# A post-norm decoder layer on one core: the quantised feed-forward unrolled into one block, on 16-bit integers and split products

## The chip, the cores and the metric

One core of one Trainium2 chip. The metric is the device time of the whole program, in microseconds (us). Engines go by the names of the profile: PE is TensorE, PEld its weight loads, DVE VectorE, ACT ScalarE, POOL GpSimd, SP SyncE (it issues the transfers here).

## The reference

`x` is 4 x 1024 rows of 256 values. The first two lines below are attention; the change is in the second and third.

```python
x = _layernorm(x + attn(x))              # 16 heads, relative positions
x = _layernorm(x + xattn(x, ctx_1024))   # one head, 154 context rows
x = _layernorm(x + ffn(x))
def act_qdq(x):                          # one scale for the whole tensor
    scale = jnp.maximum(jnp.max(jnp.abs(x)) / 32767, 1e-12)
    return jnp.clip(jnp.round(x / scale), -32768, 32767) * scale
# ffn: 256 -> 768 -> 256, weights of 4 bits with a scale for each 32
x = act_qdq(x)
up = act_qdq(x @ lpbq_dequant(w_up).T)
gate = act_qdq(x @ lpbq_dequant(w_gate).T)
sig = fixed_qdq_u16(jax.nn.sigmoid(gate))    # round to 1/65536, at most 65535/65536
gate = act_qdq(gate * sig)
o = act_qdq(gate * up)
return o @ lpbq_dequant(w_down).T
```

Each of the five `act_qdq` needs the largest absolute value of its whole tensor before the first value can be rounded. So the feed-forward falls into stages with one scale between each and the next.

## The kernel before

Line numbers are those of the profile. The self-attention fills the first 1018 us, and the diff leaves it alone. `decoder_rest` (L842) does what follows, for 8 blocks (`NBLK`) of 512 rows (`HALF`), in four `nc.Block`s, at the end of each of which all engines meet: `cross_attention` (L967), `project_gate` (L1469), `project_up` (L1592) and `down` (L1712). Within a block every engine runs its own list of instructions in order, and semaphores tie the lists. In the last three the lists are hardware loops (`Fori`), so each wait is written with `hold`: a separate wait instruction and a count on `s_held`, ahead of the instruction that it protects. In `cross_attention` the loops are unrolled in Python and a single wait is part of the instruction behind it.

**cross_attention.** Step s works on three blocks of rows at once. PE's list is: project the attention's output (`project_out`, L1336 to L1346), turn the normed rows (`turn_h`, L1355), turn the exponentials (`turn_e`, L1362 and L1365), turn the attention rows of two steps ahead (`turn_at`, L1313 to L1318), turn 512 columns of feed-forward weights (`turn_weights`, L1394), weigh the values (`weigh`, L1378 to L1381), scores (L1384 to L1390). Turns are transposes against an identity, eight of 128 x 128 for a block of rows. All turns share two pairs of PSUM banks in the order of the list `turns`: a turn begins when the copy of the last but one is done (`begin`, L1306). ACT copies each turned tile to SBUF (L1169 to L1171, `copy_e`, `copy_weights`) and does the exponentials (L1198) and the two norms' scaling. DVE adds (L1244, L1247), reduces the scores (L1257), scales and adds (L1268), and takes the largest of the finished rows (L1281). POOL adds the bias (`add_bias`, L1137), gathers tails of the exponentials (L1143), and does the small steps of the norms (`norm_rstd`, L903 to L910, behind DVE's L892 to L900). SP stores the finished rows to DRAM (L1093).

**A scale.** DVE reduces eight maxima to `top` (`largest_of`, L929), POOL reduces over the partitions (`scale_pool`, L950), DVE makes step and inverse (`scale_of`, L931 to L946). `scale_of` of the first scale stands in `project_gate`, so behind the end of the cross-attention's block.

**project_gate.** SP loads the rows again (L1488). A rounding is two steps: ACT scales and adds a magic number (L1504), DVE takes it off and scales back to values (L1536). PE turns the block (`turn`, L1565), ACT copies it (L1508), PE makes 12 fp32 products with 512 columns each for 6 banks (L1574), ACT empties the banks (L1514), DVE takes the maximum (L1540). `raw` holds the gate of all 8 blocks in fp32, `xqT` the turned rows.

**project_up.** PE makes the up products of the same `xqT` (L1708), ACT empties them to `ub` (L1649) and SP stores six of eight blocks to DRAM (L1613). Beside that the gate is rounded (ACT L1630, DVE L1664), ACT takes the sigmoid to `sg` (L1643) and rounds it (L1647), DVE clips it (L1674), multiplies (L1681) and takes the maxima of both (L1683, L1668).

**down.** For each block, the two kept in `ub` first, ACT rounds gate (L1771) and up (L1774, L1777), DVE takes the magic number off (L1794, in every second block), multiplies (L1797) and takes the maximum (L1799), while SP loads the next `ub` (L1742): the multiply stage. Behind the fifth scale ACT rounds (L1782), DVE makes values (`down_in`, L1811), PE makes 24 products of 256 columns (L1840), DVE adds the residual (`finish`, L1817) and norms, and SP writes the result (L1751, L1753): the down stage.

## Time and profile before

| | |
|---|---|
| runs of the kernel | 1586.56 us median of 3 (1586.03 to 1588.25) |
| the profiled execution, its own time | 1586.74 us |
| its span | 1585.0 us, 25411 instructions |
| mean granted clock of TensorE | 0.928 |
| PE busy | 1329.9 us (84%) |
| DVE busy | 1073.5 us (68%) |
| ACT busy | 967.9 us (61%) |
| POOL busy | 277.3 us (17%) |

The profile is of one execution. A line of a timeline is: start in us from the beginning of the span, duration in us, engine, line of the kernel, operation, output<-input with shapes, x how many such in a row were put together; in brackets how long the engine had idled before it, and what ended that. The shares are means over stages with different limits, the self-attention above all, so they say little of the last 570 us; those are read by stretches.

### The profile page before, as it was taken

Reading aid. Unit: us, or ns where it says so; the run is one execution under the profiler, and the core shown is the slowest. Engines: PE = TensorE matmul, PEld = TensorE weight load, DVE = VectorE, ACT = ScalarE, POOL = GpSimd, SP = SyncE. Lnnn points to the kernel's source line nnn. Section 1 sums busy time; section 2 is a strip of 40 time slices with the busy share of each in tenths; the row PEclk is TensorE's granted clock in tenths of the full one; section 3 lists DMA queues with packets and bytes.
Section 4 is the critical chain, followed back from the end, with each engine's and each line's share of the span. In section 5 each row is a group of like instructions: output and inputs, shape, how many; then the busy total and the mean of one; then the engine's idle time right before and its main releaser. Section 6 shows DMA issues by size and latency. Waiting matters only on the chain. (4 is left out here: it accounts for less than half of the span.)

```text
span 1585.0 us, 25411 instructions
## 1 busy us (share of the span) xinstructions
PE 1329.9 (84%) x8028; PEld 652.3 (41%) x8028; DVE 1073.5 (68%) x2571; ACT 967.9 (61%) x1652; POOL 277.3 (17%) x524
## 2 busy tenths in 40 slices
PE   5867799999999999999999999699739988600587
PEld 2433243344334433443344333278624433200576
DVE  4246678877887788778877888237623359979354
ACT  2332477777777777777777777447624478768500
POOL 2332112121212121212121211044300000000011
PEclk8989899999999999999999999899959999955799
DMA  4999786978697879787977770463121002125022
GB/s 107 258 301 303 190 235 196 253 200 235 197 251 202 234 198 251 201 230 202 248 204 225 207 243 17 139 181 111 40 80 40 13 40 119 79 80 185 0 95 90
DMA packets 264618, 264.73 MB, mean 167 GB/s; under 512 B 65934, under 2 KB 250926, under 8 KB 260398
## 3 DMA queue, kind: packets, MB, share of 16 engines
q1 hardware_dynamic: 264494, 263.21, 57.6%
q8 instruction: 61, 1.00, 0.3%
q14 instruction: 63, 0.52, 0.1%
HBM read 151.66 MB, written 110.71 MB: 166 GB/s over the span
## 5 line engine op out<-in xcount | busy, mean ns | idle before, releaser
L537 ACT ACTIVATE pr<-scoresT 128x512 f32<-128x512 f32 x1024 | 551.4, 602 | 217.0 <-PE scoresT L788 158.7
L784 PE MATMUL scoresT<-qT,kT 99*128 99x512 bf16 (+7 forms) x1408 | 358.7, 326 | 7.1 <-DMA qT<-sh 5.3
L639 DVE TENSOR_REDUCE mx<-scores_for_max 128x1 f32<-128x888 f32 (+6 forms) x448 | 301.9, 674 | 0.0
L634 DVE CUSTOM_DVE_ANT_0 junk<-scores_for_max,win 128x200 f32<-128x200 f32 (+2 forms) x512 | 180.2, 352 | 163.4 <-PE scores_for_max L759 156.0
L637 DVE TENSOR_REDUCE mx<-scores_for_max 128x1 f32<-128x64 f32 (+6 forms) x448 | 277.8, 620 | 0.0
L801 PE MATMUL attn_out<-pr,vS 128*17 128x512 f32 x2048 | 269.5, 598 | 0.1
L784 PEld LDWEIGHTS scoresT<-qT,kT 99*128 99x128 bf16 (+1 forms) x1408 | 113.7, 97 | 335.7 <-ACT rows L517 97.8
L788 PE MATMUL scoresT<-idf,win 128*128 128x128 f32 x1024 | 218.2, 274 | 0.0
L1840 PE MATMUL banks<-w_downT,work 128*128 128x256 f32 x384 | 87.5, 392 | 106.2 <-DVE work L1811 106.2
L758 PE MATMUL scores_for_max<-kX,qT 64*128 64x512 bf16 x512 | 165.4, 385 | 11.0 <-DVE mx L639 9.2
L434 POOL COPY rows<-rows 128x736 f32<-128x736 f32 x128 | 102.2, 799 | 398.6 <-ACT rows L517 398.6
L759 PE MATMUL scores_for_max<-kX,qX 64*128 64x512 bf16 x512 | 165.4, 385 | 0.0
L788 PEld LDWEIGHTS scoresT<-idf,win 128*128 128x128 f32 x1024 | 131.9, 143 | 21.8
L1840 PEld LDWEIGHTS banks<-w_downT,work 128*128 128x128 f32 x384 | 75.8, 198 | 118.3 <-issue 107.3
L1708 PE MATMUL banks<-xqT,w_upT 128*128 (+1 forms) x192 | 87.2, 609 | 18.5 <-ACT ub L1649 12.9
L1574 PE MATMUL banks<-xqT,w_gateT 128*128 128x512 f32 (+1 forms) x192 | 85.5, 603 | 0.0
L758 PEld LDWEIGHTS scores_for_max<-kX,qT 64*128 64x128 bf16 x512 | 35.8, 93 | 108.7 <-issue 61.9
L463 POOL TENSOR_TENSOR an<-ov,orec 128x256 f32<-128x256 f32 x32 | 19.9, 622 | 294.6 <-DVE orec L654 189.4
L517 ACT ACTIVATE rows<-scoresT 128x288 f32<-128x288 f32 x128 | 53.5, 418 | 24.5 <-DMA rel_table<-rows 19.3
L1540 DVE TENSOR_REDUCE amax<-raw (+1 forms) x8 | 26.8, 3353 | 60.5 <-ACT raw L1514 60.5
L1708 PEld LDWEIGHTS banks<-xqT,w_upT 128*128 128x128 f32 x192 | 36.4, 194 | 69.3 <-issue 69.2
L1514 ACT ACTIVATE raw<-banks 128x512 f32 (+1 forms) x48 | 28.7, 597 | 46.4 <-PE banks L1574 46.4
(172 smaller groups left out, 1612.7 us busy)
## 6 DMA issues: line engine op xcount, KB each, us to landing
rel_table<-rows SPq DMA_DIRECT2D x128, 512.0 KB, 4.2
win<-rel_table SPq DMA_DIRECT2D x128, 512.0 KB, 5.4
up_raw<-ub SPq DMA_DIRECT2D x6, 1536.0 KB, 5.1
ub<-up_raw SPq DMA_DIRECT2D x6, 1536.0 KB, 6.6
qT<-q_parts SPq DMA_DIRECT2D x32, 256.0 KB, 7.3
kX<-k_parts SPq DMA_DIRECT2D x64, 128.0 KB, 4.8
kT<-k_parts SPq DMA_DIRECT2D x32, 256.0 KB, 5.5
q_parts<-part SPq DMA_DIRECT2D x32, 192.0 KB, 5.5
```

Of the source, the lines that this page charges most:

```text
L434: nc.gpsimd.tensor_copy(rows[:, j, :, 0:LP], rows[:, j, :, LP:LP + 1].to_broadcast([P, G, LP])).then_inc(r_padded, 1)
L537: nc.scalar.activation(pr[:, n % NPR, h, :], bank, ACT.Exp).then_inc(t_read, 1)
L634: last = nc.vector.tensor_tensor_reduce(junk[:, n % 2, 0:z - a], bank[:, a:z], win[:, T % NW, q4, h, u:u + z - a], 1.0, NEG, ALU.add, ALU. ...
L637: last = nc.vector.tensor_reduce(mx[:, T % 2, q4, h, 0:1], bank[:, 0:a], AX.X, ALU.max)
L639: last = nc.vector.tensor_reduce(mx[:, T % 2, q4, h, 2:3], bank[:, z:L], AX.X, ALU.max)
L758: mm(psX[:, n % 2, 0:HALF], qT[0:64, q_slot(i), h, lo:lo + P], kX[0:64, i % 2, h, :], start=True, stop=True)
L759: mm(psX[:, n % 2, HALF:L], qX[64:128, i % 2, h, lo:lo + P], kX[64:128, i % 2, h, :], start=True, stop=True).then_inc(x_full, 1)
L784: last = mm(bank[:, a:e], k[0:r], q[0:r, a:e], start=(n == 0), stop=not near and n == len(pieces) - 1, skip_group_check=True)
L788: last = mm(bank[:, q4 * P:(q4 + 1) * P], side, idf[:], is_transpose=True, start=False, stop=n == len(near) - 1, skip_group_check=True)
L801: last = mm(psO[32 * h:32 * h + VW, :], vS[:, i % 2, kt, VW * h:VW * (h + 1)], pr[:, n % NPR, h, :], start=(kt == 0), stop=(kt == TL - 1))
L1708: last = nc.tensor.matmul(ps[:, m, :], wuT[:, c, m * P:(m + 1) * P], xqT[:, c, bass.ds(n, 1), :].rearrange("p a n -> p (a n)"), start=(c = ...
L1840: last = nc.tensor.matmul(ps[:, 2 * par + q // 2, (q % 2) * D:(q % 2 + 1) * D], work[:, par, m * HALF + q * P:m * HALF + (q + 1) * P], wdT ...
```

## The change

The three blocks of the feed-forward become one, `feed_forward`, unrolled in Python, with plain waits in place of `hold`. In it:

- The turn of the rows moves into the cross-attention, `turn_x(n)` behind `turn_at` of step n + 3, the last three behind the main loop; it turns the rows before they are rounded, to `xr`, [128, 2, 8, 512] in fp32. SP's store of the rows stays (the residual of the last norm needs it); the load for the gate goes. The first scale is made in the cross-attention's block.
- A rounding is one step: ACT scales and writes a 16-bit integer (`xi`, `gi`, `si`, `ui`). Steps and inverses are multiplied in where a later instruction scales anyway.
- Gate and up products are three products of type float32r on halves of the operands: rows and weights are each split into a high part (a copy of type float32r) and the rest, and low x high, high x high and high x low go to the same bank. The weights are split by POOL in the cross-attention (`split_weights`), the rows by DVE ahead of the gate (`split_rows`) and again by POOL for the up products (`split_again`), since only two blocks of halves are kept.
- All eight banks take products in turn, in place of six.
- The sigmoid is scaled by DVE into an unsigned 16-bit integer, which replaces the clip, the rounding on ACT and the taking-off.
- In the down stage the products stay fp32; the block is unrolled and double-buffered as before.
- POOL gets a spare all-reduce at the start of the cross-attention.

```diff
-        wuT = sb("w_upT", [P, 2, FI])
-        wgT = sb("w_gateT", [P, 2, FI])
+        wuh = sb("w_up_high", [P, 2, FI], F32R)
+        wul = sb("w_up_low", [P, 2, FI], F32R)
+        wgh = sb("w_gate_high", [P, 2, FI], F32R)
+        wgl = sb("w_gate_low", [P, 2, FI], F32R)
...
+            nc.gpsimd.partition_all_reduce(spare[:], neg_half[:], P, RMAX)
...
+            def split_weights(j):
+                pool.wait_ge(w_whole, j + 1)
+                nc.gpsimd.tensor_copy(high, wt[:, j % 2]).then_inc(w_high, 1)
+                pool.wait_ge(w_high, j + 1)
+                nc.gpsimd.tensor_tensor(low, wt[:, j % 2], high.bitcast(F32), ALU.subtract).then_inc(w_low, 1)
...
+                    split_weights(s - 2)
                 if s + 2 < NBLK:
...
+                if j < 6:
+                    if j >= 2:
+                        act.wait_ge(w_low, j - 1)
...
-                    copy(f"at{s + 2}", pair(atT[:]))
+                    copy(f"at{s + 2}", atT[:])
+                if 3 <= s <= NBLK:
+                    copy(f"x{s - 3}", xr[:, :, s - 3, :])
...
+            dve.wait_ge(d_am, NBLK)
+            largest_of(dve, 0)
+            scale_of(dve, 0, d_link, 0)
...
+            def turn_x(n):
+                pe.wait_ge(d_h2, n + 1)
+                to = begin(f"x{n}")
+                for c in range(2):
+                    for q in range(4):
+                        last = tr(to[:, c, q * P:(q + 1) * P], h2[:, n % 2, q, c * P:(c + 1) * P], idf[:])
+                last.then_inc(t_turned, 1)
...
+                if s >= 3:
+                    turn_x(s - 3)
...
+        xi = sb("x_int", [P, 2, NBLK, HALF], I16)
+        xh = sb("x_high", [P, 2, 2, HALF], F32R)
+        xl = sb("x_low", [P, 2, 2, HALF], F32R)
+        gi0 = sb("g_int", [P, FT * HALF], I16)
+        si = sb("s_int", [P, FT * HALF], U16T)
...
+            for n in range(NBLK - 2):
+                sp.wait_ge(f_out, M_ALL + FT * (n + 1))
+                sp.dma_start(ud[n], ub[n % 2]).then_inc(u_st[n % 2], 16)
...
+            def split_again(n):
+                pool.wait_ge(f_full, M_ALL + FT * (n - 1))
+                for c in range(2):
+                    k = 2 * n + c
+                    if k:
+                        pool.wait_ge(f_xu, k)
+                    nc.gpsimd.tensor_copy(x_one, xi[:, c, n, :]).then_inc(f_x1, 1)
+                    pool.wait_ge(f_x1, k + 1)
+                    nc.gpsimd.tensor_copy(xh[:, n % 2, c], x_one).then_inc(f_x2, 1)
+                    pool.wait_ge(f_x2, k + 1)
+                    nc.gpsimd.tensor_tensor(xl[:, n % 2, c], x_one, xh[:, n % 2, c].bitcast(F32), ALU.subtract).then_inc(f_xu, 1)
+            pool.wait_ge(f_xg, NBLK)
+            split_again(0)
+            scale_pool(pool, 1)
+            split_again(1)
+            for n in range(2, NBLK):
+                split_again(n)
+            scale_pool(pool, 2)
+            scale_pool(pool, 3)
...
+            def round_rows(n):
+                nc.scalar.activation(xi[:, :, n, :], xr[:, :, n, :], ACT.Identity, scale=inv[:, 0:1]).then_inc(f_xi, 1)
+            def empty(k, to):
+                act.wait_ge(f_full, k + 1)
+                nc.scalar.activation(to, ps[:, k % BANKS, :], ACT.Identity, scale=step[:, 0:1]).then_inc(f_out, 1)
...
+            def round_gate(n):
+                if n >= 2:
+                    act.wait_ge(f_g2, n - 1)
+                nc.scalar.activation(gi[n % 2], raw[:, n, :], ACT.Identity, scale=inv[:, 1:2]).then_inc(f_gi, 1)
...
+            def sigmoid(n):
+                act.wait_ge(f_gi, n + 1)
+                nc.scalar.activation(raw[:, n, :], gi[n % 2], ACT.Sigmoid, scale=step[:, 1:2]).then_inc(f_sig, 1)
+            def empty_up(n, first, last):
+                if first == 0 and n >= 2:
+                    act.wait_ge(u_st[n % 2], 16 * (n // 2))
+                    act.wait_ge(f_umax, n - 1)
+                for m in range(first, last):
+                    empty(M_ALL + FT * n + m, ub[n % 2][:, cols(m)])
...
+            round_rows(0)
+            round_rows(1)
+            for n in range(NBLK):
+                if n + 2 < NBLK:
+                    round_rows(n + 2)
+                for m in range(FT):
+                    empty(FT * n + m, raw[:, n, cols(m)])
+            act.wait_ge(t_inv, 2)
+            round_gate(0)
+            for n in range(NBLK):
+                sigmoid(n)
+                empty_up(n, 0, FT // 2)
+                if n + 1 < NBLK:
+                    round_gate(n + 1)
+                empty_up(n, FT // 2, FT)
+            for k, n in enumerate(ORDER):
+                if k == 0:
+                    act.wait_ge(t_inv, 3)
+                if k >= 2:
+                    act.wait_ge(f_o, k - 1)
+                nc.scalar.activation(gi[k % 2], raw[:, n, :], ACT.Identity, scale=inv[:, 2:3]).then_inc(f_g2i, 1)
+                if k == 0:
+                    act.wait_ge(t_inv, 4)
+                if n not in KEPT:
+                    act.wait_ge(u_ld[n % 2], 16 * (n // 2 + 1))
+                nc.scalar.activation(ui[k % 2], ub[n % 2], ACT.Identity, scale=inv[:, 3:4]).then_inc(f_ui, 1)
+            act.wait_ge(t_inv, 5)
+            for n in range(NBLK):
+                nc.scalar.activation(raw[:, n, :], raw[:, n, :], ACT.Identity, bias=magic[:, 0:1], scale=inv[:, 4:5]).then_inc(o_r, 1)
...
+            def split_rows(n):
+                dve.wait_ge(f_xi, n + 1)
+                if n >= 2:
+                    dve.wait_ge(f_full, FT * (n - 1))
+                nc.vector.tensor_copy(xh[:, n % 2], xi[:, :, n, :]).then_inc(f_xh, 1)
+                dve.wait_ge(f_xh, n + 1)
+                nc.vector.tensor_tensor(xl[:, n % 2], xi[:, :, n, :], xh[:, n % 2].bitcast(F32), ALU.subtract).then_inc(f_xg, 1)
...
+            def largest_up(n):
+                dve.wait_ge(f_out, M_ALL + FT * (n + 1))
+                largest(3, n, ub[n % 2], f_umax)
+            split_rows(0)
+            split_rows(1)
+            for n in range(NBLK):
+                dve.wait_ge(f_out, FT * (n + 1))
+                if n + 2 < NBLK:
+                    split_rows(n + 2)
+                largest(1, n, raw[:, n, :], f_gmax)
+            dve.wait_ge(f_gmax, NBLK)
+            largest_of(dve, 1)
+            scale_of(dve, 1, f_link, 0)
+            dve.wait_ge(t_inv, 2)
+            nc.vector.tensor_scalar(coarse[:, 0:1], step[:, 1:2], 1.0 / U16, None, ALU.mult).then_inc(f_link, 1)
+            for n in range(NBLK):
+                dve.wait_ge(f_sig, n + 1)
+                nc.vector.tensor_scalar(si[:], raw[:, n, :], U16, None, ALU.mult).then_inc(f_si, 1)
+                dve.wait_ge(f_si, n + 1)
+                nc.vector.tensor_tensor(raw[:, n, :], gi[n % 2], si[:], ALU.mult).then_inc(f_g2, 1)
+                if n:
+                    largest_up(n - 1)
+                dve.wait_ge(f_g2, n + 1)
+                largest(2, n, raw[:, n, :], f_g2max)
+            dve.wait_ge(f_g2max, NBLK)
+            largest_of(dve, 2)
+            largest_up(NBLK - 1)
+            scale_of(dve, 2, f_link, 2, coarse[:, 0:1])
+            dve.wait_ge(f_umax, NBLK)
+            largest_of(dve, 3)
+            scale_of(dve, 3, f_link, 5)
+            dve.wait_ge(t_inv, 4)
+            nc.vector.tensor_tensor(coarse[:, 1:2], step[:, 2:3], step[:, 3:4], ALU.mult).then_inc(f_link, 1)
+            for k, n in enumerate(ORDER):
+                dve.wait_ge(f_ui, k + 1)
+                nc.vector.tensor_tensor(raw[:, n, :], gi[k % 2], ui[k % 2], ALU.mult).then_inc(f_o, 1)
+                dve.wait_ge(f_o, k + 1)
+                largest(4, n, raw[:, n, :], f_omax)
...
+            down_in(0)
+            down_in(1)
+            for n in range(NBLK):
+                finish(n)
+                if n + 2 < NBLK:
+                    down_in(n + 2)
...
+                for m in range(FT):
+                    k = first + FT * n + m
+                    if k >= BANKS:
+                        pe.wait_ge(f_out, k - BANKS + 1)
+                    cols = slice(m * P, (m + 1) * P)
+                    terms = [(w[:, c, cols], v[:, n % 2, c]) for w, v in ((low, xh), (high, xh), (high, xl)) for c in range(2)]
+                    for t, (w, v) in enumerate(terms):
+                        last = mm(ps[:, k % BANKS, :], w, v, start=(t == 0), stop=(t == len(terms) - 1))
+                    last.then_inc(f_full, 1)
+            for n in range(NBLK):
+                pe.wait_ge(f_xg, n + 1)
+                project(0, n, wgh, wgl)
+            for n in range(NBLK):
+                pe.wait_ge(f_xu, 2 * n + 2)
+                project(M_ALL, n, wuh, wul)
+            pe.wait_ge(f_out, 2 * M_ALL)
+            for n in range(NBLK):
+                pe.wait_ge(o_q, n + 1)
+                if n >= 4:
+                    pe.wait_ge(l_sum, 2 * NBLK + n - 3)
```

## Rows read from the trace of the kernel before

**Rows 1.** Stretches: busy us and operations of PE, PEld, DVE, ACT, POOL; PEclk, DMA, GB/s.

```profile
1184.65:1274.30 89.65, 89.65 (x241) 41.99 (x240) 27.53 (x13) 41.52 (x60) 0.00 (x0) 0.98 0.10 30
1290.01:1394.60 104.59, 77.20 (x175) 31.90 (x173) 101.53 (x39) 81.79 (x69) 0.00 (x0) 0.95 0.22 91
1408.16:1473.40 65.24, 0.00 (x0) 0.00 (x0) 60.36 (x20) 48.42 (x17) 0.00 (x0) 0.50 0.45 161
1480.08:1573.80 93.72, 87.50 (x384) 75.76 (x384) 42.85 (x98) 17.77 (x7) 11.94 (x28) 0.93 0.23 73
1066.00:1165.00 99.00, 80.44 (x484) 66.60 (x481) 59.08 (x218) 61.20 (x147) 38.66 (x68) 0.91 0.25 75
```

**Rows 2.** The timeline of one step of the cross-attention, PE and ACT.

```profile
1081.83 2.36 PE L1390 MATMUL banks<-kq,h1T 128*128 128x154 f32 x16
...
1090.82 1.02 ACT L1171 ACTIVATE atT<-banks 128x1024 f32<-128x1024 f32 x1 [0.50 <-PE banks L1318]
...
1093.94 2.13 PEld L1390 LDWEIGHTS banks<-kq,h1T 128*128 128x128 f32 x16 [0.33 <-issue]
```

**Rows 3.** The timeline of PE: two bf16 passes, gate products, a turn.

```profile
600.10 0.39 PE L758 MATMUL scores_for_max<-kX,qT 64*128 64x512 bf16 x1
...
600.32 0.38 PE L758 MATMUL scores_for_max<-kX,qT 64*128 64x512 bf16 x1
...
1184.65 12.43 PE L1574 MATMUL banks<-xqT,w_gateT 128*128 128x512 f32 x24
...
1197.78 10.46 PE L1574 MATMUL banks<-xqT,w_gateT 128*128 128x512 f32 x24
...
1208.09 1.04 PE L1565 MATMUL banks<-ident_f,hb 128*128 128x128 f32 x8
```

**Rows 4.** The timeline of POOL in the self-attention: a subtraction and a copy.

```profile
23.13 1.15 POOL L430 TENSOR_TENSOR part<-rem,part 128x512 bf16<-128x512 f32 x1 [20.75 <-ACT part L505]
...
69.23 0.80 POOL L434 COPY rows<-rows 128x736 f32<-128x736 f32 x1
```

**Rows 5.** The timeline where POOL changes between its own operations and the all-reduce.

```profile
1030.07 2.35 POOL L1137 TENSOR_TENSOR xt<-xt,bot 128x1024 f32<-128x1024 f32 x1 [11.08 <-DMA xt<-x]
...
1035.84 1.22 DVE L1247 TENSOR_TENSOR h<-banks,xt 128x1024 f32<-128x1024 f32 x1 [21.19 <-PE banks L1346]
...
1167.62 0.16 DVE L929 TENSOR_REDUCE top<-amax 128x1 f32<-128x8 f32 x1 [2.22 <-PEq L976]
...
1174.31 0.38 POOL L950 PARTITION_ALL_REDUCE top_all<-top  x1 [12.36 <-issue]
...
1278.95 0.35 POOL L950 PARTITION_ALL_REDUCE top_all<-top  x1 [104.27 <-DVE top L929]
...
1496.56 0.38 DVE L900 BATCH_NORM_AGGREGATE mean_var<-stats 128x2 f32<-128x6 f32 x4
...
1504.06 0.25 POOL L905 TENSOR_SCALAR rstd<-mean_var 128x4 f32<-128x4 f32 x1 [30.02 <-issue]
```

**Rows 6.** The timeline of ACT at the start and the end of the up stage.

```profile
1285.80 1.28 ACT L1643 ACT_TABLE_LOAD   x1
...
1384.63 2.86 ACT L1647 ACTIVATE sg<-sg,magic 128x3072 f32<-128x3072 f32 x1 [4.03 <-DVE sg L1674]
...
1387.39 1.55 ACT L1649 ACTIVATE ub<-banks 128x512 f32<-128x512 f32 x3
```

**Rows 7.** The timeline of DVE in a block of the up stage.

```profile
1355.82 1.75 DVE L1674 TENSOR_SCALAR sg<-sg 128x3072 f32<-128x3072 f32 x1
...
1362.47 3.35 DVE L1681 SCALAR_TENSOR_TENSOR raw<-sg,raw 128x3072 f32 x1
...
1366.06 3.35 DVE L1683 TENSOR_REDUCE amax<-raw  x1 [0.24 <-DVE raw L1681]
```

**Rows 8.** The down stage: PE in the timeline, then the last link of the chain.

```profile
1509.91 10.32 PE L1840 MATMUL banks<-w_downT,work 128*128 128x256 f32 x40 [6.18 <-DVE work L1811]
...
1509.91 63.86 PE banks L1840 x288
```

More of the change, by code:

```diff
@@ L1055, in cross_attention @@
         turns += [f"w{j}" for j in range(NBLK - 1, W_GROUPS)]
+        turns += [f"x{n}" for n in range(NBLK - 2, NBLK)]
         turn_of = {name: n for n, name in enumerate(turns)}
@@ L1240, in _ @@
                         copy_weights(j)
+            for n in range(NBLK - 2, NBLK):
+                copy(f"x{n}", xr[:, :, n, :])
         @block.vector
@@ L1717, in down @@
-def down(nc, sem, hold, tokens, h2d, ud, wdT, magic, coarse, t_coarse, step, inv, t_inv, ps, raw, ub, amax,
-         largest_of, scale_of, scale_pool, l_sum, norm_stats, norm_rstd, norm_apply, out):
-    with ExitStack() as ctx:
-        work = ctx.enter_context(nc.sbuf_tensor("work", [P, 2, FT * HALF], F32))
-        res = ctx.enter_context(nc.sbuf_tensor("res", [P, 2, 4, D], F32))
-        p_ld = [sem(f"p_ld{j}") for j in range(2)]
-        p_g = sem("p_g")
-        p_gi = sem("p_gi")
-        p_odd = sem("p_odd")
-        p_u = sem("p_u")
-        p_o = sem("p_o")
-        p_a = sem("p_a")
+            for n in range(NBLK - 2, NBLK):
+                turn_x(n)
@@ L1736, in down, with wait, rows_of @@
         block = ctx.enter_context(nc.Block())
+        def wait(eng, s, value):
+            eng.wait_ge(s, value)
+        def rows_of(t, n):
+            return t[n].rearrange("(q p) d -> p q d", p=P)
         @block.sync
         def _(sp):
[L1740 to L1746 removed]
@@ L1779, in _ @@
-            run_kept_first(act, multiply)
-            act.wait_ge(t_inv, NSC + 1)
-            with act.Fori(0, NBLK) as n:
-                nc.scalar.activation(flat(raw, n), flat(raw, n), ACT.Identity, bias=magic[:, 0:1], scale=inv[:, 4:5]).then_inc(o_r, 1)
+            def round_rows(n):
[3 more added lines that the diff above has]
+                nc.scalar.activation(to, ps[:, k % BANKS, :], ACT.Identity, scale=step[:, 0:1]).then_inc(f_out, 1)
@@ L1832, in _, with project @@
+            down_in(0)
[4 more added lines that the diff above has]
+                    down_in(n + 2)
         @block.tensor
         def _(pe):
-            def products(n, par, before):
-                hold(pe, o_q, n + 1)
-                if before:
-                    hold(pe, l_sum, 2 * NBLK + n - 1)
+            mm = nc.tensor.matmul
+            def project(first, n, high, low):
+                for m in range(FT):
[7 more added lines that the diff above has]
+                    last.then_inc(f_full, 1)
```

483 lines of the change are left out of this document (142 added, 341 removed).

## The prediction

> **What bounds the kernel now.** I read the share of each stage first, then the order of time inside each, then what ended the waits. The change leaves the first 1018 us (the self-attention) as they are, so the question is the rest. The table of stretches [rows 1] shows five kinds of work there. In the cross-attention PE is busy 80 of 99 us, more than any other engine. In the gate products it is busy all 89.65 us. In the up products DVE is busy 101.5 of 104.6 us and PE only 77. In the multiply stage PE has nothing and DVE 60 of 65 us. In the down products PE is busy 87.5 of 93.7 us. Between them lie hand-offs, in which nearly all engines wait for one scale. So three stages end with PE and two with DVE, and what each edit is worth is read in its own stage.
>
> **Cross-attention, with the rows turned there.** A step lasts 12.1 us, from scores to scores [rows 2]. Eight transposes end to end take 1.04 us, so eight more cost 8 x 0.11 = 0.9 us of PE per step [rows 3]. The turn of the weights now also waits for the copy of `at` (1.02 us), beside which the new turn runs: 0.4 more. Steps 3 to 7 give 5 x 1.3, step 8 about 1.0: **+7.5**. Ends: 5.3 (transposes alone) and 11 (each copy shows as well). ACT's extra copy lies beside PE's work, and so do POOL's weight splits, 0.6 + 1.15 each [rows 4]; without that cover each would cost its own length, up to 1.8 a step. The two last turns and the store of the rows run beside the scale below.
>
> **POOL's turn between its own operations and the all-reduce.** The scale of the rows shows a price with no engine behind it [rows 5]: `top` starts at 1167.62, the all-reduce only at 1174.31. The first small operation after the all-reduces starts at 1504.06, though its input was there at 1497. Between all-reduces there is none: that at 1278.95 starts as its `top` ends. I read this as 6.6 to 6.8 us for each turn of POOL from the one kind to the other, paid when POOL comes to it; an instruction's own single wait lies behind it, so it can pass beside a wait, which a separate held wait forbids. The Trainium skill, GPSIMD Engine Reference, Instruction dispatch, says that the first call to a freshly loaded kernel costs about 6 us that no instruction shows; by its figure each turn is 0.7 us cheaper than I take. The new spare all-reduce at 1019 then brings two turns, to 1033, and the first bias ends at 1035.4 in place of 1032.4. DVE's first sum starts at 1035.84 and waits for PE: cost 0, or a few us if the turns are longer.
>
> **Hand-off to the gate.** Before: POOL's last small operation ends at 1161.95 (1174.31 - 12.36), the first product starts at 1184.65 [rows 3]: 22.7. After: POOL turns at once, beside the second norm (6.6), all-reduce 0.4, step and inverse 0.5, end of the block 0.5, rounding of 1024 columns 1.1 (from 2.86 for 3072 [rows 6]), copy 0.7 and subtraction 1.2 on DVE (from 1.75 and 3.35 for 3072 [rows 7]), semaphores 0.5: 11.5. The load, the second rounding step and the turn have gone. **-11.2**.
>
> **Gate.** Now a product is two instructions of 0.43 us for 512 columns (24 in 10.46 [rows 3]); with eight transposes a block takes 11.2. After: 36 products a block of the new type. The trace doesn't show it; the nearest rows are bf16 at 0.22 us (600.10 to 600.32) and the 4-byte instruction at 0.43. I take 0.22: a full product takes two instructions of twice 0.22, which is four combinations of halves, and the change writes out three of these four itself, on values cut to one half. Against it speaks that a 4-byte transpose takes 0.11 for 128 columns, the rate of 0.43. The Trainium skill, FP8 and Floating Point Precision, TensorE Precision Notes, counts true fp32 as four passes, high and low of both operands, and the trace's 4 x 0.215 agrees; by it a product is 0.215 and the gate 1.4 us shorter than I take. The weights' loads hide, since transposes with a load each follow at 0.11. 288 x 0.22 = 63.4, and 2.0 for the start at the lower clock, as the first block pays today (12.43 against 10.46): 65.4 against 89.65, **-24.3**. DVE (0.7 + 1.2 + 3.35) and ACT (1.1 + 6 x 0.6) stay under the 7.9 of PE. If the loads show, 0.25 to 0.27 a product, +9 to +14.
>
> **Hand-off to the up stage.** POOL starts its first split one block before the gate's end G, at G - 7.9: two copies 1.2, a turn 6.8, subtraction 1.2, the other half 2.6; done at G + 4. Then the turn back 6.6 and the all-reduce, G + 11.0, though `top` is there at G + 4.2. Inverse G + 11.5, rounding 2.9, table 1.3, sigmoid 2.9 [rows 6]: DVE starts at G + 18.8. Today it is 1290.01 - 1274.30 = 15.7: **+3.1**.
>
> **Up stage.** DVE per block after: scaling 1.75, a product of 3.35 behind a gap of 0.15 to 0.24, two maxima of 3.3 [rows 7]: 11.7. One scaling (1.8) has gone; the product keeps its length, as its output stays 4 bytes wide. First block 9.1, then 7 x 11.7: 91.0 against 104.6, **-13.6**. ACT (2.8 + 2.9 + 6 x 0.6) and PE (7.9) stay under it. New is POOL beside DVE, splitting again: 2 x (0.6 + 0.6 + 1.15) and waits, 5.2 us a block [rows 4]. No row shows the two side by side on such work. Ends: 0, and all 5.2. I take 0.5, as DVE's maxima (6.6 of 11.7) leave POOL room: **+3.5**.
>
> **To the multiply stage.** DVE's first product waits for two passes of ACT, not three, and no block ends: 13.6 becomes 10.1, **-3.5**. **Multiply stage.** DVE 3.5 + 3.4 a block; ACT's 2 x 2.8 is under it and the loads of `ub` have two blocks to land. 55.3 against 65.2, **-9.9**. The hand-off to the down stage stays.
>
> **Down stage.** POOL now meets its turn ahead of the wait for the statistics, so the 6.18 us in which PE stands at 1509.91 go. The unrolled code may shorten the block (63.86 / 6 = 10.64 [rows 8]); for that I take 1.0: **-7.2**. Next late is DVE, 9.1 of 10.6 a block, no bound yet.
>
> **Sum.** 7.5 - 11.2 - 24.3 + 3.1 - 13.6 + 3.5 - 3.5 - 9.9 - 7.2 = -55.6. The profiled execution took 1586.74 (span 1585.0), 0.2 over the median of the runs, too little to matter: 1586.7 - 55.6 = 1531.
>
> **Rivals.** *A: a product of the new type streams like any 4-byte operand, 0.43 us.* For it: every 4-byte row does. Against: the count of halves. Gate 288 x 0.21 = +60.4. Up: a block is 15.5 us of PE, over DVE's 11.7; from G + 18.8, with eight banks ahead, 40 groups of 2.58 end at G + 122 and the last maximum at G + 126, where it was G + 117: +9.5. Total 1601, slower. With the up stage the point from which it decides is 0.40 us a product.
> *B: DVE and POOL shut each other out, so that all 5.2 us of POOL's block stand in DVE's way.* Against: POOL needs under half of the block. 7 x 4.7 = +33: 1564. The Trainium skill, SBUF — State Buffer, SBUF: two separate sides, speaks for it: VectorE with two SBUF inputs or in a two-port mode and GpSimd exclude each other for a whole instruction. No row here shows that.
> *C: the 6.7 us are paid once per kind, not at each turn.* Then the spare call has paid: the rows' scale comes 3 us earlier, the gate's 6.3: 1522. Against: 1504.06 is an operation that POOL had done all through the cross-attention.
> *D: it doesn't do what it says*: the splits wait for buffers and the stages keep their length, 1587.
>
> **How the numbers follow.** Forecast case 0.66, A 0.18, B 0.08, C 0.06, D 0.02. The time is that of the first. Its own range is 1518 to 1550: cross-attention -2 to +3.5, product 0.215 to 0.27, POOL 0 to 1 us a block, hand-offs 3 either way. The range for all, 1516 to 1566, takes in B and C and leaves out A and D, 0.20. A measurement of this kernel can tell about 0.2% (3 us) from no change. Faster by more: 0.66 + 0.08 + 0.06 = 0.80; the same 0.02; slower 0.18.
>
> **What would show it.** 36 single products of a block in 7.9 us and a gate stage of 64 to 67; the all-reduce of the gate's scale 6 us behind its `top`; DVE 11.7 us a block in the up stage, 6.9 in the multiply stage, with no waits for ACT or PE; no hole of PE in the down stage; a cross-attention step of 13.4. Products 0.43 us apart would make it wrong outright; DVE operations that start late or last longer than 3.35 us while POOL splits would be B.

## The result, and the profile after

Median of 4 runs 1525.44 us (1523.96 to 1526.34) against 1587.4 us of the kernel before, measured beside it; ratio 0.9608, 95% interval 0.9591 to 0.9625: faster by 3.9%. The profiled execution took 1525.12 us, its span 1523.2. Forecast were 1531 and a range of 1516 to 1566.

The span falls apart into stages by the same marks in both traces: POOL's first memset, the end of its last small operation in the cross-attention, PE's first and last gate product, DVE's first scaling, the reduction to `top` behind the up stage, the first product of the multiply stage, the next reduction to `top`, PE's first and last product of the down stage, the end.

| stage | before, us | after, us | difference | forecast |
|---|---|---|---|---|
| self-attention, up to the memset | 1018.08 | 1016.72 | -1.4 | 0 |
| cross-attention | 143.87 | 148.97 | +5.1 | +7.5 |
| hand-off to the gate | 22.70 | 10.07 | -12.6 | -11.2 |
| gate | 89.65 | 67.87 | -21.8 | -24.3 |
| hand-off to the up stage | 15.71 | 17.87 | +2.2 | +3.1 |
| up stage | 104.55 | 96.24 | -8.3 | -13.6 + 3.5 |
| hand-off to the multiply stage | 13.60 | 9.73 | -3.9 | -3.5 |
| multiply stage | 65.27 | 53.35 | -11.9 | -9.9 |
| hand-off to the down stage | 6.65 | 6.43 | -0.2 | 0 |
| down stage | 93.68 | 86.03 | -7.7 | -7.2 |
| tail | 11.24 | 9.92 | -1.3 | 0 |
| span | 1585.0 | 1523.2 | -61.8 | -55.6 |

The stretches of the changed kernel that answer to [rows 1], the cross-attention last again (columns as there):

```profile
1175.76:1243.63 67.87, 67.83 (x288) 55.61 (x288) 36.22 (x21) 37.09 (x54) 1.22 (x2) 0.96 0.00 0
1261.50:1357.70 96.20, 63.66 (x252) 50.92 (x252) 93.44 (x31) 67.05 (x62) 54.66 (x40) 0.82 0.28 109
1367.47:1420.78 53.31, 0.00 (x0) 0.00 (x0) 53.04 (x16) 38.84 (x14) 0.00 (x0) 0.50 0.49 177
1427.25:1513.28 86.03, 86.03 (x384) 74.95 (x384) 42.93 (x98) 17.80 (x7) 11.94 (x28) 0.97 0.25 80
1064.70:1165.70 101.00, 85.42 (x539) 72.44 (x537) 58.20 (x217) 64.54 (x149) 49.64 (x80) 0.96 0.25 74
```

The bounds are where they were: PE in the gate (67.83 of 67.87 us) and in the down stage (no hole any more), DVE in the up stage (93.44 of 96.20) and in the multiply stage, where it now has next to no gap. New is POOL in the up stage, 54.66 us busy beside DVE.

PE in a step of the cross-attention, to be read against [rows 2], and the first products of the gate stage beside some at full clock, against [rows 3]; the timeline:

```profile
1080.50 2.36 PE L1414 MATMUL banks<-kq,h1T 128*128 128x154 f32 x16
1089.29 1.04 PE L1423 MATMUL banks<-ident_f,h 128*128 128x128 f32 x8
1090.66 0.63 PE L1437 MATMUL banks<-ident_f,wn 128*128 128x128 f32 x4 [0.33 <-ACT atT L1180]
1094.01 2.36 PE L1414 MATMUL banks<-kq,h1T 128*128 128x154 f32 x16
...
1175.76 1.22 PE L1748 MATMUL banks<-x_high,w_gate_low 128*128 128x512 f32 x2 [5.86 <-DVE x_low L1663]
1176.78 1.05 PE L1748 MATMUL banks<-x_high,w_gate_high 128*128 128x512 f32 x2
...
1185.40 0.62 PE L1748 MATMUL banks<-x_high,w_gate_high 128*128 128x512 f32 x2
1185.86 0.62 PE L1748 MATMUL banks<-x_low,w_gate_high 128*128 128x512 f32 x2
```

A step is 13.51 us (1080.50 to 1094.01) where it was 12.11: the turn at L1423 and 0.33 us of wait for the copy of `at` ahead of the next one. A pair of split products starts every 0.455 us: 0.227 a product, no longer 0.436 for each half of an fp32 one. The first five pairs run at the lower of the clock's two levels, 0.85 a pair; PE had stood still for 5.86 us before them. The granted clock was 0.50 in 1176 to 1180 and 1.00 from 1181 on.

POOL's timeline around the two hand-offs, against [rows 5]:

```profile
1165.49 0.20 POOL L904 TENSOR_TENSOR shift<-shift,rstd 128x4 f32<-128x4 f32 x1
1171.51 0.38 POOL L946 PARTITION_ALL_REDUCE top_all<-top  x1 [5.82 <-issue]
1235.58 0.61 POOL L1579 CAST xT_normed<-x_int 128x512 f32<-128x512 int16 x1 [63.69 <-PE banks L1748]
1236.25 0.61 POOL L1581 CAST x_high<-xT_normed 128x512 fp32r<-128x512 f32 x1
1243.86 1.25 POOL L1583 TENSOR_TENSOR x_low<-xT_normed,x_high 128x512 fp32r<-128x512 f32 x1 [7.00 <-issue]
...
1253.65 0.38 POOL L946 PARTITION_ALL_REDUCE top_all<-top  x1 [5.84 <-issue]
1253.91 0.67 POOL L1579 CAST xT_normed<-x_int 128x512 f32<-128x512 int16 x1
1254.64 0.61 POOL L1581 CAST x_high<-xT_normed 128x512 fp32r<-128x512 f32 x1
1261.94 2.44 POOL L1583 TENSOR_TENSOR x_low<-xT_normed,x_high 128x512 fp32r<-128x512 f32 x1 [6.69 <-issue]
1264.45 3.62 POOL L1579 CAST xT_normed<-x_int 128x512 f32<-128x512 int16 x1
```

All four turns are there, released by nothing ("issue"): 5.8 us toward an all-reduce, 6.7 and 7.0 toward a subtraction, none before a cast. The gate's `top` is ready at 1247.89, the all-reduce comes at 1253.65. The trace also has a mark for a turn, in the view by source line (a q marks an instruction of the engine's sequencer; then count, ns at least, median and most, first and last start):

```profile
L946 POOLq MODIFY_POOL_CONFIG  x6: 8/8/11, 1165.9 to 1323.2; - x6
L1583 POOLq MODIFY_POOL_CONFIG  x4: 9/10/11, 1236.9 to 1255.3; - x4
L899 POOLq MODIFY_POOL_CONFIG  x2: 83/83/83, 1421.4 to 1421.4; - x2
```

They come two at a time, at the start of each turn, and none stands before a cast or between two all-reduces. So each turn can be placed in time: two that cost nothing began at 1323.2 and at 1421.4, each right behind the last operation of the other kind, and passed while POOL waited, the second for statistics that released it only at 1443.98.

The last two lines of POOL's timeline show something else: a subtraction of 1.27 us takes 2.44 and a cast of 0.61 takes 3.62.

DVE in the same stretch, and then in the multiply stage, against [rows 7]:

```profile
1261.50 1.76 DVE L1686 TENSOR_SCALAR s_int<-raw 128x3072 uint16<-128x3072 f32 x1 [6.90 <-ACT raw L1616]
1263.29 4.30 DVE L1688 TENSOR_TENSOR raw<-g_int,s_int 128x3072 f32<-128x3072 int16 x1
1267.63 3.35 DVE L1666 TENSOR_REDUCE amax<-raw 128x1 f32<-128x3072 f32 x1
...
1285.30 1.82 DVE L1686 TENSOR_SCALAR s_int<-raw 128x3072 uint16<-128x3072 f32 x1 [2.45 <-ACT raw L1616]
1287.16 4.33 DVE L1688 TENSOR_TENSOR raw<-g_int,s_int 128x3072 f32<-128x3072 int16 x1
...
1374.13 3.35 DVE L1704 TENSOR_TENSOR raw<-xT_normed,x_int 128x3072 f32<-128x3072 int16 x1
1377.52 3.35 DVE L1666 TENSOR_REDUCE amax<-raw 128x1 f32<-128x3072 f32 x1
1380.79 3.35 DVE L1704 TENSOR_TENSOR raw<-g_int,s_int 128x3072 f32<-128x3072 int16 x1
```

Put beside POOL's rows, the two take turns. POOL's subtraction, begun at 1261.94, ends 1.1 us after DVE's scaling does (1263.26); DVE's product, begun at 1263.29, lasts 0.94 longer than 3.36, about to that subtraction's end; POOL's cast then ends 0.5 us after the product (1267.59). DVE's maxima are never longer than 3.35. DVE's wait of 2.45 us at 1285.30 goes back to POOL too. PE is through with the first block of up products at 1257.9 and gets the second only behind POOL's second split:

```profile
1270.14 1.22 PE L1748 MATMUL banks<-x_high,w_up_low 128*128 128x512 f32 x2 [12.24 <-POOL x_low L1583]
```

The down stage, the last link of the chain of waits, against [rows 8]:

```profile
1427.25 86.05 PE banks L1765 x384
```

### The profile page after: what moved, and what is told of

Its sections match the earlier page's. It is cut to its first block and busy times, and to the rows that moved or that the text cites. A ratio compares the mean times of both kernels' runs of the same rounds, so it can differ in the third digit from the quotient of the medians.

```text
span 1523.2 us, 24859 instructions
## 1 busy us (share of the span) xinstructions
PE 1296.6 (85%) x8220; PEld 691.8 (45%) x8220; DVE 1065.6 (70%) x2570; ACT 938.9 (62%) x1640; POOL 349.3 (23%) x585
## 5 line engine op out<-in xcount | busy, mean ns | idle before, releaser
L1765 PE MATMUL banks<-w_downT,xT_normed 128*128 128x256 f32 x384 | 86.0, 388 | 86.9 <-DVE xT_normed L1716 86.9
L791 PEld LDWEIGHTS scoresT<-idf,win 128*128 128x128 f32 x1024 | 131.9, 142 | 21.8
L1765 PEld LDWEIGHTS banks<-w_downT,xT_normed 128*128 128x128 f32 x384 | 75.0, 196 | 97.9 <-issue 87.3
L1666 DVE TENSOR_REDUCE amax<-raw 128x1 f32<-128x3072 f32 x24 | 80.3, 3347 | 8.1 <-ACT raw L1604 7.7
L433 POOL TENSOR_TENSOR part<-rem,part 128x512 bf16<-128x512 f32 x32 | 36.8, 1155 | 95.5 <-ACT part L508 95.5
L735 PE MATMUL scoresT<-embS,qT 96*128 96x72 bf16 x512 | 38.1, 197 | 21.9 <-ACT rows L520 10.2
L1748 PE MATMUL banks<-x_high,w_up_low 128*128 128x512 f32 x96 | 32.9, 426 | 23.1 <-POOL x_low L1583 19.7
L1604 ACT ACTIVATE raw<-banks,step 128x512 f32<-128x512 f32 x48 | 33.1, 689 | 30.8 <-PE banks L1748 30.8
```

Source lines behind the costliest of these rows:

```text
L791: last = mm(bank[:, q4 * P:(q4 + 1) * P], side, idf[:], is_transpose=True, start=False, stop=n == len(near) - 1, skip_group_check=True)
L1666: nc.vector.tensor_reduce(amax[:, k, n:n + 1], src, AX.X, ALU.max, apply_absolute_value=True).then_inc(done, 1)
L1765: last = mm(ps[:, 2 * b + q // 2, q % 2 * D:(q % 2 + 1) * D], work[n % 2][:, m * HALF + q * P:m * HALF + (q + 1) * P], wdT[:, m, :], start ...
```

## The experiments

All are edits of the changed kernel. The start of the cross-attention moved between 1014.9 and 1020.0 us from profile to profile, with the same self-attention ahead of it, which is as much as some of the effects; so the stages decide, and the totals stand beside them. The runs were made on several chips, each beside the kernel before (medians of 1587.3 to 1589.3 us), so totals are compared by their ratios to it. The profiled executions, in us:

| kernel | memset | cross | to gate | gate | to up | up | multiply | down | median of the runs |
|---|---|---|---|---|---|---|---|---|---|
| changed | 1016.72 | 148.97 | 10.07 | 67.87 | 17.87 | 96.24 | 53.35 | 86.03 | 1525.44 |
| same_again | 1018.74 | 149.70 | 10.28 | 68.04 | 18.04 | 96.23 | 53.35 | 86.06 | 1528.45 (one run) |
| reduce_first | 1014.93 | 150.03 | 10.06 | 68.17 | 12.28 | 107.39 | 53.35 | 85.13 | 1531.97 |
| up_whole | 1020.03 | 148.96 | 10.13 | 67.93 | 12.21 | 90.52 | 53.35 | 84.94 | 1516.63 |
| all_whole | 1015.85 | 149.73 | 8.90 | 84.27 | 12.20 | 90.52 | 53.35 | 86.12 | 1529.18 |
| two_splits | 1016.08 | 149.53 | 10.11 | 68.13 | 17.88 | 92.00 | 53.35 | 84.91 | 1521.93 |
| gate_two | 1017.78 | 149.77 | 10.05 | 46.36 | 20.88 | 95.57 | 53.35 | 85.66 | 1507.41 (one run) |
| late_turns | 1016.76 | 145.53 | 10.12 | 67.70 | 18.31 | 95.96 | 53.35 | 85.84 | 1521.34 |
| both | 1017.97 | 144.32 | 10.87 | 67.23 | 12.21 | 90.52 | 53.35 | 84.57 | 1510.58 |
| held_stats | 1018.91 | 149.76 | 10.74 | 67.83 | 17.98 | 96.17 | 53.35 | 93.78 | 1537.13 |
| held_max | 1018.59 | 150.09 | 10.35 | 68.01 | 18.41 | 96.10 | 54.24 | 85.45 | 1529.31 (one run) |
| no_spare | 1017.11 | 150.03 | 9.85 | 68.26 | 17.94 | 95.62 | 53.34 | 84.83 | 1527.11 |

**The spread.**

> The changed kernel unaltered, for the spread of the stages: the cross-attention's first memset was at 1016.72 us in the first profile and between 1014.9 and 1020.0 in the runs since, with the same self-attention ahead of it. If that start belongs to the kernel's code, it is within 0.5 us of 1016.7 again; if to the execution, it is anywhere in that range. Stages from the gate to the multiply stage within 0.4 us of the first profile, the down stage between 84.5 and 86.2.

The memset came 2 us later with the same code, so the start belongs to the execution. The cross-attention moves by 0.7 us here and by 1.1 (148.97 to 150.09) over the kernels that leave it as it is, the down stage by more than 1 between the kernels, the stages from the gate to the multiply stage by 0.2 here. A difference of 1 us or less in the first two, or below 2 us of a total, says nothing here.

**The order of POOL's work.**

```diff
-            split_again(0)
             scale_pool(pool, 1)
+            split_again(0)
```

> The gate's all-reduce is put ahead of POOL's first split of the rows for the up products; nothing else moves. Theory (POOL pays 6 to 7 us whenever it changes between its own subtractions and the all-reduce, at the place where it comes to it): the all-reduce starts 0.2 us behind its top (near 1248.0 in place of 1253.7) since the one before it was an all-reduce too; ACT rounds the gate and DVE's first scaling starts at about 1256 in place of 1261.5. But the first halves are ready 10 us later, at 1257.5 and 1260, so PE's first up block starts near 1260 in place of 1247.9, ACT stands in front of its banks with the rounding of block 1 queued behind them, and DVE waits for the second sigmoid until about 1277. Sum: +3 us against the changed kernel, 0 to +6. Rival 1 (the hand-off alone counts, the up products have room): -5 to -6. Rival 2 (the turns are an accident of that place and are paid once): within 1 us, and the all-reduce still 6 us behind its top.

The hand-off became 5.6 us shorter and the up stage 11.2 longer, together +5.6 (ratio to the kernel before 0.9646, 0.9628 to 0.9665). POOL, PE and DVE in its timeline:

```profile
1247.64 0.35 POOL L946 PARTITION_ALL_REDUCE top_all<-top  x1 [76.49 <-DVE top L923]
1256.16 2.19 POOL L1583 TENSOR_TENSOR x_low<-xT_normed,x_high 128x512 fp32r<-128x512 f32 x1 [6.94 <-issue]
1258.41 3.61 POOL L1579 CAST xT_normed<-x_int 128x512 f32<-128x512 int16 x1
...
1264.10 1.22 PE L1748 MATMUL banks<-x_high,w_up_low 128*128 128x512 f32 x2 [20.95 <-POOL x_low L1583]
...
1278.86 1.79 DVE L1686 TENSOR_SCALAR s_int<-raw 128x3072 uint16<-128x3072 f32 x1 [13.91 <-ACT raw L1616]
```

An all-reduce behind an all-reduce starts as its `top` ends; the turn comes at the first subtraction. That is the theory; both rivals fall. The sum came out at the upper end of what was expected: DVE's product held up the cast at 1258.41, PE began at 1264.1, not 1260, and DVE waited 13.9 us for the second sigmoid. So the order in the changed kernel, which makes the all-reduce wait, is the better of the two.

**Whole fp32 operands for the up products.** POOL only casts; the weights are copied whole.

```diff
-                for c in range(2):
...
-                    nc.gpsimd.tensor_tensor(xl[:, n % 2, c], x_one, xh[:, n % 2, c].bitcast(F32), ALU.subtract).then_inc(f_xu, 1)
+                nc.gpsimd.tensor_copy(xu[:, n % 2], xi[:, :, n, :]).then_inc(f_xu, 1)
...
+                    if low is None:
+                        terms = [(high[:, c, cols], xu[:, n % 2, c]) for c in range(2)]
```

> The up products go back to whole fp32 operands (2 products a bank in place of 6 of the split type), the gate products stay split. POOL then only casts the integers to fp32 (1.2 us a block) and subtracts nothing in the feed-forward; its weight splits of the up weights go too. Theory (turns of POOL and its subtractions beside DVE are what the up stage pays, PE has room there): the all-reduce follows its top at once, DVE starts 5.6 us earlier (1255.9), DVE's wait of 2.45 us in the third block goes, products of 4.3 and 3.65 us become 3.36, worth 3 to 4; PE takes 10.5 us a block against DVE's 11.6 and stays under it. Sum -11.5 us, -9 to -13: 1514. Rival (the split is what makes the up stage fast, as PE would be the bound without it): PE's 84 us of fp32 and the eight banks push DVE: 0 to +8.

The two stages fell by 5.7 and 5.7, 11.4 together. The ratio is 0.9550 (0.9530 to 0.9569). The profiled execution is shorter by 9.1 us alone, since its memset came 3.3 us later and its down stage was 1.1 shorter. Its timeline, POOL, PE and DVE:

```profile
1251.43 0.36 POOL L946 PARTITION_ALL_REDUCE top_all<-top  x1 [11.39 <-DVE top L923]
...
1246.85 28.48 PE L1746 MATMUL banks<-x_whole,w_up_whole 128*128 128x512 f32 x66
...
1268.21 2.12 DVE L1681 TENSOR_SCALAR s_int<-raw 128x3072 uint16<-128x3072 f32 x1 [0.41 <-ACT raw L1611]
1270.37 3.36 DVE L1683 TENSOR_TENSOR raw<-xT_normed,s_int 128x3072 f32<-128x3072 int16 x1
```

PE goes from the last gate product into the up products without a gap, and neither DVE nor ACT waits for it in the up stage. With only casts in between, the all-reduce at 1251.43 starts as its `top` ends, without a turn. Every product of DVE takes 3.36; one scaling is longer, 2.12, at the only place where POOL's cast (1267.68, 1.04 us) lies just ahead of it. The split had bought nothing in this stage and cost 11.4 us.

**Both whole.** The same for the gate, and DVE casts without subtracting.

```diff
-                nc.vector.tensor_copy(xh[:, n % 2], xi[:, :, n, :]).then_inc(f_xh, 1)
-                dve.wait_ge(f_xh, n + 1)
-                nc.vector.tensor_tensor(xl[:, n % 2], xi[:, :, n, :], xh[:, n % 2].bitcast(F32), ALU.subtract).then_inc(f_xg, 1)
+                nc.vector.tensor_copy(xg[:, n % 2], xi[:, :, n, :]).then_inc(f_xg, 1)
```

> Gate and up products both in whole fp32, no product is split; the integers, the one block and the turns in the cross-attention stay. Theory (a split product is 6 instructions of 0.227 us, a whole one 4 of 0.436, so a gate block goes from 8.2 to 10.5 us and PE remains the bound): gate stage 86 us in place of 68, +17 against the kernel that has the up products alone whole (1516.6), less 1.2 for a subtraction on DVE ahead of the first product: 1532. Rival (the emptying by ACT and the splits and maxima of DVE set the gate's pace as much as PE): +10 or less.

Gate 84.27 against 67.93, +16.3, and 1.2 less in the hand-off to it: the split is worth 15.1 us there. The gate's products in the view by groups, ahead of a further 4 of the up stage:

```profile
L1741 PE MATMUL banks<-x_gate,w_gate_whole 128*128 128x512 f32 x192 | 84.2, 601 | 4.7 <-DVE x_gate L1653 4.7
```

The total was 1529.18 (0.9635, 0.9616 to 0.9654), 3 below the 1532 forecast. Without any split product the integers, the one block and the moved turns together give 3.65% where the whole change gives 3.92%.

**The splits beside DVE.** Only the first two stay.

```diff
-            for n in range(2, NBLK):
-                split_again(n)
```

> Against the changed kernel only this: POOL splits rows again for the first two blocks of the up products alone, the other six take the halves that are there. The values of six up blocks are left out in this way; the work of every other engine stays. Theory (DVE and POOL shut each other out for a whole instruction): from the second block's product on DVE's scaling takes 1.75 and its product 3.36 us in every block, in place of up to 2.5 and 4.3; DVE's wait of 2.4 us in the third block, which comes from the late second split, stays. Up stage -3.1 us. Rival (the 16-bit operands, or ACT beside it, make the products longer): 4.3 and 3.65 stay, 0.

The up stage fell by 4.24, more than 3.1. DVE there:

```profile
1263.52 4.30 DVE L1686 TENSOR_TENSOR raw<-g_int,s_int 128x3072 f32<-128x3072 int16 x1
...
1284.10 1.76 DVE L1684 TENSOR_SCALAR s_int<-raw 128x3072 uint16<-128x3072 f32 x1 [1.31 <-ACT raw L1614]
1285.90 3.36 DVE L1686 TENSOR_TENSOR raw<-g_int,s_int 128x3072 f32<-128x3072 int16 x1
```

The first product, beside which POOL still subtracts, stays at 4.30; every later one, of the same integers, takes 3.36. The rival falls. In the changed kernel the excess over 3.36 and 1.75 adds up to 4.0 us over eight blocks, 3.1 of it behind the first product; the other 1.1 is the wait in the third block, 1.31 in place of 2.45, part of which had come from DVE and POOL holding each other up too.

**Two products in place of three in the gate.**

```diff
+                    pairs = ((high, xh), (high, xl)) if first == 0 else ((low, xh), (high, xh), (high, xl))
```

> Against the changed kernel only this: a gate bank takes 4 split products (high x high and high x low) in place of 6; the product of the weights' low half with the rows' high half is left out, so the gate's values are coarser. Theory (PE bounds the gate stage by 0.227 us an instruction): 192 x 0.227 = 43.6 and 2.6 at the lower clock: gate stage 46 in place of 67.9. Rival (ACT's 6 emptyings and its rounding, 4.7 to 5.3 us a block, or DVE's 5.3, take over before): 48 to 52.

46.36: PE's 0.227 an instruction holds down to 5.44 us a block, with DVE's 5.3 just under it. The hand-off to the up stage grew by 3.0, since POOL starts its split one block ahead of the end and that block is now 2.7 us shorter, while the turn takes as long as before (7.25 us for 7.00): the turn is a fixed piece of time, as the theory has it.

**The turns of the rows.** Buffers hold the first normed blocks (two of them, in the kernel `both` three), and their turns go behind that of the last block but one.

```diff
-            for n in range(NBLK - 2, NBLK):
+            for n in [NBLK - 2] + list(range(DEFER)) + [NBLK - 1]:
                 turn_x(n)
```

> Against the changed kernel only this: the turns of the first two blocks of rows go from steps 3 and 4 of the cross-attention to PE's gap before the last turn. Theory: two steps fall from 13.5 to 12.1 us, nothing is added in the gap: -2.8 us, the last small operation of POOL 2.8 us earlier counted from the first one of the cross-attention. Rival (the cost only moves to the gap): 0 to -1.

-3.4 us, where 2.8 were expected (the stage itself moves by up to 1.1); steps 3 and 4 took 12.12 us each. With three blocks and the whole up products:

> The up products whole as in the run before, and the turns of the first three blocks of rows moved out of steps 3 to 5 of the cross-attention, where PE has no gap, to the 6.8 us in which PE waits for the last normed rows (with buffers that hold those rows). Theory (a turn costs 1.4 us in a step that PE fills and nothing in a gap): steps 3 to 5 fall from 13.5 to 12.1 us, the last turn starts no later relative to the last norm, total -4.2 us against the kernel with whole up products (1516.6), that is 1512.4. Rival (ACT's four copies, 4.1 us, and the turns at the lower clock delay the last norm behind them, so that the cost only moves): -1 to -2.

-4.6 in the cross-attention against up_whole; 0.7 was given back in the hand-off, as POOL's turn took 6.6 in this execution. 1510.58 us (0.9518, 0.9498 to 0.9537): 0.9% below the changed kernel by the two ratios, and the fastest kernel that computes the whole layer. PE in the gap:

```profile
1158.88 1.98 PE L1434 MATMUL banks<-ident_f,h 128*128 128x128 f32 x16 [0.33 <-ACT xT_normed L1185]
1164.53 1.97 PE L1434 MATMUL banks<-ident_f,h 128*128 128x128 f32 x8 [3.67 <-ACT h L910]
```

3.67 us of the gap are still free behind the three moved turns.

**How a wait is written.** Two kernels, one for POOL's wait for the first statistics of the down stage, one for DVE's waits in the multiply stage:

```diff
+            def hold(eng, s, value):
+                eng.wait_ge(s, value)
+                eng.sem_inc(s_held, 1)
-                norm_rstd(pool, 2 * NBLK + n, n % 2, wait)
+                norm_rstd(pool, 2 * NBLK + n, n % 2, wait if n else hold)
```

> One wait alone is written as before the change: POOL's wait for the statistics of the first block of the down stage is a separate instruction with a count behind it, ahead of the first small operation. Theory (the turn of POOL stands behind a separate wait and ahead of an instruction's own): the first small operation starts 6 to 7 us later than its statistics, PE gets a hole of 6 to 7 us behind the second block, total +6.5 us (+5 to +8). Rival (the hole of the kernel before came from the hardware loops and their many held waits): within 1 us of the changed kernel.

The down stage took 93.78, +7.75, what it had taken before the change. POOL and PE:

```profile
1455.15 0.25 POOL L899 TENSOR_SCALAR rstd<-mean_var 128x4 f32<-128x4 f32 x1 [30.07 <-issue]
...
1460.55 64.14 PE L1769 MATMUL banks<-w_downT,xT_normed 128*128 128x256 f32 x288 [5.80 <-DVE xT_normed L1720]
```

The mark of the turn, in this run:

```profile
L899 POOLq MODIFY_POOL_CONFIG  x2: 11/11/11, 1447.7 to 1447.8; - x2
```

The statistics were there at 1447.5, the turn begins at 1447.7, where it began at 1421.4 in the changed kernel, and the operation starts 7.65 us behind the statistics; PE's hole is 5.8, and 1.9 us more go into its products, with a granted clock of 0.66 in 1455 to 1465 where the changed kernel has 1.00. The profiled execution is longer by 11.4 us in all, of which 2.2 are the later memset and 1.5 lie in the cross-attention and the hand-off behind it, within their spread. The rival, the loops, falls.

```diff
                 dve.wait_ge(f_o, k + 1)
+                dve.sem_inc(s_held, 1)
                 largest(4, n, raw[:, n, :], f_omax)
```

> Against the changed kernel only this: in the multiply stage DVE's two waits of a block are written as a separate wait with a count behind it, as before the change. Theory (a separate wait on what the engine itself has just written costs 0.24 us and loses the overlap of 0.08): the maximum starts 0.24 us behind the end of the product, 0.2 later than now, and the next product loses its overlap: 8 x 0.2 to 8 x 0.5, stage 55 to 57.5 in place of 53.35. Rival (the stage got shorter by the integers and the missing scaling alone): 53.3 to 53.7.

54.24, +0.9: neither. The maximum starts 0.14 us behind the product (1371.39 + 3.36 to 1374.89), 0.11 later than in the changed kernel, and the next product keeps its overlap. My 0.24 was read off rows inside the hardware loops; what makes the gap longer there was not tried.

**The spare all-reduce.**

```diff
-            nc.gpsimd.partition_all_reduce(spare[:], neg_half[:], P, RMAX)
```

> The spare all-reduce at the start of the cross-attention is left out. Theory (each change of kind costs, and at the start PE waits for weights anyway): the first bias starts at about 1030 in place of 1032, the scale of the rows still waits 5.8 us for POOL's turn behind its last small operation, total within 1.5 us. Rival (the first all-reduce loads something once, which the spare one has paid ahead): the scale of the rows comes 5 us or more later, total +5 or more.

The medians lie 1.7 us apart, where 1.5 was the bound, and the ratios 0.0009, which is 1.4 us: within the spread. The rows' scale waits 5.60 us for its turn without the spare one, 5.82 with it. POOL's first bias is done at 1031.3 in place of 1034.3, and nobody waited for it.

## Why the prediction was right, point by point

- **The sum.** -61.8 against -55.6, all in the direction and nearly in the size of each step. 2.7 us of the difference are the self-attention's start and the tail, which no step of mine explains. The errors of the table's rows have both signs, +4.3 in the gate and the up stage and -10.5 in the rest, so part of the closeness is luck. The four bounds that I gave for the forecast case add up to 1521 to 1555, not 1518 to 1550. What the eight banks and the rounding in one step are worth by themselves was not tested.
- **Cross-attention, +5.1 for +7.5.** The mechanism was right, 1.40 us in each of steps 3 to 5 for my 1.3. The size was off in steps 6 to 8, for which I took 1.3, 1.3 and 1.0: they cost 0.6, 0.3 and 0 (from the starts of the scores, in step 8 of the last products). I had multiplied a full step's price by the number of steps, but from step 6 on no attention rows are turned, so the wait of 0.33 for their copy can't occur. In steps 7 and 8 PE also waits 3.2 and 4.1 us for the exponentials, as long as before the change, and works at the lower clock behind the wait. In step 7 of the kernel before (first line, granted clock 0.50 in 1138 to 1140) that time went to weighing the values; now the turn of the rows stands in it (0.50 in 1141 to 1143), and the weighing runs at full clock, 1.4 us shorter:

```profile
1138.09 3.32 PE L1378 MATMUL banks<-vx,eT 128*128 128x256 f32 x8
...
1140.91 1.92 PE L1423 MATMUL banks<-ident_f,h 128*128 128x128 f32 x8
...
1143.26 1.89 PE L1402 MATMUL banks<-vx,eT 128*128 128x256 f32 x8
```

- **Hand-off to the gate, -12.6 for -11.2.** The links were the ones named; `top` is ready at 1169.3 and the all-reduce at 1171.5, so the turn still ends last there, by 2.2 us.
- **POOL's turns.** "6.6 to 6.8 us for each turn" measured 5.8 toward the all-reduce and 6.7 and 7.0 back in the two hand-offs, 6.5 and 7.5 around the spare all-reduce. Rival C is refuted by reduce_first and no_spare; that a turn lies behind a separate wait and ahead of an instruction's own is shown by held_stats, by the length and by the mark at 1447.7 for 1421.4. The Trainium skill, GPSIMD Engine Reference, Instruction dispatch, gives about 6 us for the first call to a freshly loaded kernel with no instruction to show for it: the traces agree with the size and with the bare time behind the mark, and add that here each change of kind pays it again.
- **Gate, -21.8 for -24.3.** A product took 0.227, not 0.22 (288 x 0.007 = 2.0), and the low clock at the start cost 2.5 (67.87 less 288 x 0.227), not 2.0. Rival A (0.43) is refuted. What makes the 0.227 stays open.
- **Up stage, -8.3 for -10.1.** The 3.5 for POOL beside DVE were 4.0. The reason I gave, that the maxima leave POOL room, held in every block; and rival B's mechanism is at work, at the forecast's price: the two do shut each other out, shown by two_splits. I had set its price as all of POOL's work, while only what meets a scaling or a product counts. The Trainium skill, SBUF — State Buffer, SBUF: two separate sides, has this rule, with the operation that started first keeping the port to its end; by this rule a maximum with one input at its usual speed is free, and the trace agrees (all 16 took 3.34 to 3.35 us). The step that failed is "ACT and PE stay under it": in the third block DVE waits 2.45 us, since POOL's second split is done only at 1270.1, PE's second block starts then, and ACT stands before its banks with the next rounding queued behind; two_splits leaves 1.31 of that wait and up_whole none. The rest of the stage held: 90.52 us in up_whole, where next to nothing of either cost is left, for 91.0.
- **Hand-off to the up stage, +2.2 for +3.1**: each link came within 1 us. That this part of the change loses time was forecast; that it could be had back by giving up the split there was not seen, though PE's 77 of 104.6 us [rows 1] say it.
- **Multiply stage, -11.9 for -9.9.** A block took 6.66, not 6.9: the maximum starts 0.03 behind the product and overlaps the next one by 0.08. held_max gives 0.9 of the 2.0 to the way in which the waits are written.
- **Down stage, -7.7 for -7.2.** The hole of 6.18 was POOL's turn, as said; the clock that PE loses behind such a hole, 1.9 us in held_stats, is the part that I had put down to unrolled code.

## What to carry to other kernels

Before a faster form of a product is spread over several stages, ask in each of them whether PE ends last: here the same split won 15.1 us in the gate and lost 11.4 in the up stage, by the work that it laid on another engine. Group POOL's operations by kind, and where a change of kind can't be avoided, put it where POOL would have waited anyway, with a wait that belongs to the instruction itself. And an extra piece of work costs its length only in the steps in which its engine has no gap: move it to the one that has.

## What the runs showed of the hardware that was not expected

- In the up stage DVE's operations with two SBUF inputs (the product) and its scaling from fp32 to 16-bit did not run beside POOL's casts and subtractions: the one that came second was longer by what was left of the first, less about 0.15 us (casts of 0.61 us took up to 3.62, products of 3.36 up to 4.33). Maxima took 3.34 to 3.35 us beside them.
- POOL's casts need no turn in either state; between subtractions or the norms' small operations and the all-reduce there is one each time: 5.6 to 6.6 us toward the all-reduce, 6.6 to 7.6 toward a subtraction behind a cast, over all runs. Two instructions of its sequencer, MODIFY_POOL_CONFIG, mark the start, also where the turn is hidden beside a wait.
- The same kernel's self-attention ended up to 2 us apart in two executions, and the down stage's 384 products took 84.6 to 86.1 us from kernel to kernel with the same instructions.
